# Second wide attention: GpSimd adds the two key halves of each head's weights, and the sums' product reads the added columns

## Chip, cores and metric

One core of one Trainium2 chip. The metric is device time in microseconds of one execution, median of the runs.

## The reference, cut to what matters

The kernel computes four transformer blocks on 16 sequences of 256 tokens with 128 features. The change touches the third block's attention (16 heads of 64 features, no mask):

```python
qkv = data @ W_qkv + b_qkv                    # q, k, v: [n, 256, 16, 64]
scores = jnp.einsum('nqhd,nkhd->nhqk', q, k)
attention = jax.nn.softmax(scores / 8, axis=3)
out = jnp.einsum('nhql,nlhd->nqhd', attention, v).reshape(n, l, 1024)
x = x + out @ W_out + b_out
```

The softmax is computed as weights P = exp(score/8 − max/8), the product P·V, and separately the sum of P over the keys; the output product is scaled by the reciprocal of that sum.

## The kernel before, in words

The program is a list of eight stages, each with one function per engine (`pe`, `act`, `dve`, `pool`, `sp`); the engines run their instruction lists independently and meet in semaphores. The stages are: first wide attention (`Wide`, kind 0, causal), a feed-forward net, a narrow attention, a gated net, the second wide attention (`Wide`, kind 2, s = 4, the one changed; its instructions lie at about 1,515 to 2,164 us of the profiled execution), a mixture of experts, a narrow attention, a last net.

**Units and ticks.** `Wide` cuts the work into 64 units: unit g = 4b + u holds heads 4u to 4u+3 of sequence b. The function `ticks` (line 97) writes one order for all engines by hand: a unit starts every 4 ticks, and in each tick every live unit does the part whose number `k` it has reached (`self.tk`, kind 2: "turn" 0 and 1, "v" 2, "mx" 4 and 5, "mT" 7, "st" 8 and 9, "pv" 11, "sT" 12, "out" 13). Within a tick, items are sorted by `rank` (kind 2: "turn" first part 0, "sT" 1, most others 2, "turn" second part 3, "mT" 4, dispatch 5); among equals the older unit comes first. So in one tick unit g−1 is at "out" (13) and unit g at its second "st" (9), both with rank 2. Every engine walks this one list, each doing its own share of a part.

**One unit.** TensorE makes q and k (turned), v, the score maxima ("mx") and their transpose ("mT"), then the scores with keys on partitions and queries on columns ("st", two heads per part, into PSUM [128 keys, 2 x 256 columns]: columns 0:256 are keys 0 to 127, columns 256:512 keys 128 to 255). ScalarE (line 589) writes P = exp(...) of each head as a 128x512 tile, six buffers `P` in turn. At "pv", `pe_pv` (line 438) makes P times V into `pv` (eight products, two heads side by side in the array) and then the sums' product into `sm`: eight products of `one` (128x32 of ones) with a 128x256 half of a head's P, four heads side by side, two key halves added up in PSUM. An f32 product stands in the profile as two records, so both products have 16. ScalarE copies `pv` to `OT` (line 596) and `sm` to `S` (line 599), TensorE transposes S ("sT"), VectorE takes the reciprocal (line 699). At "out", `pe_out` makes the output product from OT and `wO` into two tiles Y, VectorE scales each into a tile T (line 708), and GpSimd adds the four quarters of T into the residual XR, one after the other, each waiting for the one before (`pool_sum`, line 813; the adds are at line 825). 

**Other work in this stage.** Per sequence: statistics (VectorE lines 2419, 2421; their roots on GpSimd, lines 2426, 2428), the normalised tiles z (VectorE line 2434), the output bias added to XR (`pool_bias`, GpSimd line 811, in the tick of a "prep" with k = 3, which rank puts ahead of units), and the dispatch of the mixture of experts running behind: its own statistics and tiles zd (VectorE line 1919), gate, ranks, and two indirect DMAs issued by GpSimd (line 1973).

**Ordering between ScalarE and TensorE.** The line ahead of the exp lets ScalarE overwrite a P buffer once the sums' product of the unit that last used it is done (`filled("sm", ...)`). `take` hands out PSUM banks from a ring of eight in TensorE's order. GpSimd had no part in P in this stage.

Of the kernel before, what the change touches and what calls it, by code (L numbers as in the profile page):

```python
# [7 lines left out]
ALU = mybir.AluOpType  # L8
ACT = mybir.ActivationFunctionType
F32 = mybir.dt.float32  # L10
# [117 lines left out]
class Wide:  # L128
# [9 lines left out]
    def __init__(self, K, s, kind, loads=(), behind=None):  # L138
        self.K, self.s, self.kind = K, s, kind
        self.causal = kind == 0  # L140
        if kind == 0:
            first, last, unit = 8, 9, 23
            self.tk = {"qk": 0, "turn": 6, "mx": 9, "v": 12, "mT": 15, "st": 17, "pv": 20, "sT": 21, "out": 22}
        else:
            first, last, unit = 6, 5, 14
            self.tk = {"turn": 0, "v": 2, "mx": 4, "mT": 7, "st": 8, "pv": 11, "sT": 12, "out": 13}
        self.apart = (self.tk["st"] - self.tk["mx"]) // 4
        self.zT_at, self.sn_at = (6, 8) if kind == 0 else (4, 99)
        items = []
        for b in range(NSEQ):  # L150
            items.append((16 * b, 0, "prep", (b,), last))
            for u in range(4):
                items.append((16 * b + first + 4 * u, 1, "unit", (b, u), unit))
        if behind is not None:
            behind.ring = self.G
            items += [(16 * b + first + 12 + unit, 2, "behind", (behind, b), behind.PARTS) for b in range(NSEQ)]
        items += [(at, 3, "load", (ld,), ld.parts) for at, ld in loads]
        self.order = ticks(items, self.rank)
        sb = K.scratch
        self.zT = [sb(f"zT{s}_{i}", [128, 512], F32R) for i in range(3)]  # L160
        self.QH, self.QL, self.KH, self.KL = (
            [sb(f"{n}{s}_{i}", [128, 2, 256], F32R) for i in range(4)] for n in ("QH", "QL", "KH", "KL"))
        self.MT = [sb(f"MT{s}_{i}", [128, 256], F32R) for i in range(2)]
        self.KB = sb(f"KB{s}", [128, 8, 256] if kind == 0 else [128, 2, 128], F32R)
        self.OT = [sb(f"OT{s}_{i}", [128, 2, 256], F32) for i in range(2)]
        self.z = [sb(f"z{s}_{i}", [128, 2, 128], F32) for i in range(4 if kind == 0 else 2)]
        self.V = [sb(f"V{s}_{i}", [128, 2, 4, 64], F32) for i in range(4)]
        self.w = 384 if self.causal else 512
        self.P = [sb(f"P{s}_{i}", [128, self.w], F32) for i in range(6)]
        self.S = [sb(f"S{s}_{i}", [128, 256], F32) for i in range(2)]  # L170
        self.T = [sb(f"T{s}_{i}", [128, 2, 2, 2, 128], F32) for i in range(2)]
        self.rs = [sb(f"rs{s}_{i}", [128, 8], F32) for i in range(2)]
        self.one = sb(f"one{s}", [128, 128], F32)
        self.hi_in, self.one_in, self.summed, self.z_hi, self.kb_in = (
            K.sem(f"{n}{s}") for n in ("hi_in", "one_in", "summed", "z_hi", "kb_in"))
        if kind == 0:
            self.raw = [sb(f"raw{s}_{i}", [128, 512], F32) for i in range(6)]
            self.sqr = [sb(f"sqr{s}_{i}", [128, 512], F32) for i in range(3)]
            self.sm = [sb(f"sm{s}_{i}", [128, 64], F32) for i in range(4)]
            self.ss = [sb(f"ss{s}_{i}", [128, 48], F32) for i in range(4)]  # L180
            self.sn = [sb(f"sn{s}_{i}", [128, 64], F32) for i in range(2)]
            self.pn = [sb(f"pn{s}_{i}", [128, 2, 96], F32R) for i in range(2)]
            self.pnT = [sb(f"pnT{s}_{i}", [96, 256], F32R) for i in range(2)]
            self.nvs = sb(f"nvs{s}", [96, 2, 1040], F32R)
            self.nvo = sb(f"nvo{s}", [96, 16, 32], F32R)
            self.on = sb(f"on{s}", [128, 128], F32R)
            self.sqs, self.unitq, self.nul, self.pnull, self.rec, self.m_sm, self.nvs_in, self.snl = (
                K.sem(f"{n}{s}") for n in ("sqs", "unitq", "nul", "pnull", "rec", "m_sm", "nvs_in", "snl"))
        else:
            self.beff = sb(f"beff{s}", [1, 128], F32)  # L190
            self.bo = sb(f"bo{s}", [1, 128], F32)
            self.bias = sb(f"bias{s}", [128, 128], F32)
            self.bo_in = K.sem(f"bo_in{s}")
        K.end_scratch()
# [243 lines left out]
    def pe_pv(self, pe, g, u):  # L438


        K, s, kind, V = self.K, self.s, self.kind, self.V[g % 4]
        pv, sm = (K.ps.take(pe, self.G, name, s, g) for name in ("pv", "sm"))
        pe.wait_ge(self.one_in, 1)
        if kind == 0:
            pe.wait_ge(self.nvs_in, 4)
            pe.wait_ge(*K.ps.read("mT", s, g))
            for pr in range(2):
                c = 256 * u + 128 * pr
                K.acc(pv[:, 256 * pr:256 * pr + 256], self.nvs[:, 0, c:c + 128], self.pnT[g % 2][:, :], start=pr == 0)
            K.acc(sm[:, 0:256], self.nvo[:, 4 * u:4 * u + 4, :].rearrange("p h c -> p (h c)"), self.pnT[g % 2][:, :],  # L450
                  start=True)
        pe.wait_ge(*K.ps.read("v", s, g))
        for h in range(4):
            pe.wait_ge(*K.ps.read("st", s, g, h))
        P = [self.P[(4 * g + h) % 6] for h in range(4)]
        for pr in range(2):
            for kt, q, c, w in self.blocks():
                for par in range(2):
                    p = K.acc(pv[64 * par:64 * par + 64, 256 * pr + q:256 * pr + q + w], V[:, kt, 2 * pr + par, :],
                              P[2 * pr + par][:, c:c + w], start=kind == 2 and kt == 0 and pr == 0)  # L460
        p.then_inc(K.ps.full_of("pv", s, g), 1)
        for kt, q, c, w in self.blocks():
            for h in range(4):
                p = K.acc(sm[32 * h:32 * h + 32, q:q + w], self.one[:, 0:32], P[h][:, c:c + w],
                          start=kind == 2 and kt == 0)
        p.then_inc(K.ps.full_of("sm", s, g), 1)

    def pe_out(self, pe, g, u):
# [63 lines left out]
    def act_unit(self, ac, b, u, k):  # L532
        K, s, g, e, kind = self.K, self.s, 4 * b + u, ac.e, self.kind
        n = self.part("qk", k)
        if n is not None:
            at = 2 * g + n
# [8 lines left out]
        n = self.part("turn", k)  # L545
# [37 lines left out]
        if n is not None:  # L583
            for h in (2 * n, 2 * n + 1):
                at = 4 * g + h
                if at >= 6:
                    ac.wait_ge(*K.ps.filled("sm", s, (at - 6) // 4))
                ac.wait_ge(*K.ps.filled("st", s, g, h))
                e.activation(self.P[at % 6][:, :], K.ps.ap("st", s, g, h)[:, 0:self.w], ACT.Exp, bias=0.0,  # L589
                             scale=1.0 if kind == 0 else 0.125).then_inc(K.ps.out_of("st", s, g, h), 1)  # L590
# [191 lines left out]
    def pool(self, po):  # L782
        K, s, e = self.K, self.s, po.e
        K.stage_free(po, s)
        e.memset(self.one[:, :], 1.0).then_inc(self.one_in, 1)
        if self.kind == 0:
            for pn in self.pn:
                e.memset(fv(pn[:, :, :]), 0.0).then_inc(K.pn_in, 1)
        for name, a, k in self.order:
            if name == "prep":  # L790
                n = K.nb[s] + (4 if self.kind == 0 else 2) * a[0]
                if k == 0 or (k == 2 and self.kind == 0):
                    for i in range(2):
                        K.pool_rstd(po, n + k + i)
                if k == 3 and self.kind == 2:
                    self.pool_bias(po, a[0])
            elif name == "behind":
                a[0].pool(po, a[1], k)
            elif name == "unit":
                if self.kind == 0:  # L800
                    self.pool_unit(po, 4 * a[0] + a[1], k)
                if self.part("out", k) is not None:
                    self.pool_sum(po, *a)
            elif name == "load":
                a[0].pool(po, k)

    def pool_bias(self, po, b):
        K, x = self.K, self.K.XR[:, 2 * b:2 * b + 2, :]
        po.wait_ge(K.zs, K.nb[self.s] + 2 * b + 2)
        po.wait_ge(*K.ps.read("bias"))  # L810
        self.biased = po.step(po.e.tensor_tensor(x, x, self.bias[:, :].unsqueeze(1).to_broadcast([128, 2, 128]), ALU.add))

    def pool_sum(self, po, b, u):

# [1890 lines left out]
```

## Time and profile before

| | |
|---|---|
| median of 3 runs | 2811.08 us (2804.03 to 2811.64) |
| profiled execution, own time | 2820.46 us |
| its span | 2818.1 us |
| TensorE (PE) busy | 2493.8 us, 88% |
| VectorE (DVE) busy | 1690.2 us, 60% |
| ScalarE (ACT) busy | 1487.5 us, 53% |
| GpSimd (POOL) busy | 1455.3 us, 52% |

The rows below come from that one profiled execution; its time lies 9.4 us above the median of the runs. Matmul ends are modelled in a profile, so the distance between starts is the safer measure on PE. PE is the matmul, PEld the load of its weights. "L825" is line 825 of the kernel before. Times are microseconds unless marked ns.

### The profile page before, as it was taken

What the parts mean: (1) busy time and instruction counts of PE and PEld (TensorE: products, weight loads), DVE (VectorE), ACT (ScalarE), POOL (GpSimd) and SP (SyncE); (2) the same over time, 40 slices, a digit from 0 to 9 for tenths busy, and PEclk for the clock granted to TensorE, in tenths of its full rate; (3) what the DMA queues carried; (4) which work ended last, traced back from release to release, by engine and by line L of the source; (5) the groups of instructions that cost most, each with busy time, mean ns of one, the idle gap of its engine ahead of it and who ended that gap; (6) DMA issues with size and microseconds to landing.
All of it is one profiled execution on the core that took longest, in us unless ns stands there. A gap on an engine that the chain in (4) does not pass through costs nothing. (4 is left out here: it accounts for less than half of the span.)

```text
span 2818.1 us, 63055 instructions
## 1 busy us (share of the span) xinstructions
PE 2493.8 (88%) x24681; PEld 1914.1 (68%) x24681; DVE 1690.2 (60%) x4432; ACT 1487.5 (53%) x3177; POOL 1455.3 (52%) x2283
## 2 busy tenths in 40 slices
PE   4999999999988688889998999999996858888855
PEld 3888888888865455557777777777775745555533
DVE  4677777777757577645444666666664115555548
ACT  3666666666644476644444555555553324555531
POOL 4687777777756544434332444444443144554454
PEclk9999999999999699999999999999998977999975
DMA  3790000000000100000000000000000630000000
GB/s 107 227 325 25 2 2 2 2 2 2 2 2 1 49 2 2 2 1 21 1 1 3 3 5 5 4 6 5 6 4 16 186 97 7 7 7 3 1 1 30
DMA packets 22969, 82.68 MB, mean 29 GB/s; under 512 B 4082, under 2 KB 10868, under 8 KB 21652
## 3 DMA queue, kind: packets, MB, share of 16 engines
q1 hardware_dynamic: 19524, 71.44, 7.9%
q0 software_dynamic: 3152, 7.21, 0.8%
q8 instruction: 198, 3.24, 0.5%
q14 instruction: 95, 0.78, 0.1%
HBM read 71.44 MB, written 46.79 MB: 42 GB/s over the span
## 5 line engine op out<-in xcount | busy, mean ns | idle before, releaser
L825 POOL TENSOR_TENSOR XR<-XR,T 128x256 f32<-128x256 f32 x512 | 375.3, 733 | 441.5 <-DVE T L708 411.4
L2410 PE MATMUL ps<-P,V 128*64 128x256 f32 (+3 forms) x4096 | 341.0, 356 | 14.0 <-DVE O L1293 11.9
L589 ACT ACTIVATE P<-ps 128x384 f32<-128x384 f32 (+1 forms) x512 | 250.4, 542 | 188.6 <-PE ps L2410 188.6
L1283 DVE TENSOR_REDUCE qa<-ps 128x2 fp32r<-128x512 f32 x256 | 176.3, 689 | 219.8 <-PE ps L2410 219.7
L1206 ACT ACTIVATE P<-ps 128x768 f32<-128x768 f32 x256 | 207.5, 811 | 150.7 <-PE ps L2410 149.3
L2410 PEld LDWEIGHTS ps<-P,V 128*64 128x64 f32 (+1 forms) x4096 | 187.8, 125 | 126.1 <-issue 27.2
L2410 PE MATMUL ps<-mk,identb 128*128 128x256 bf16 (+1 forms) x1024 | 203.8, 302 | 60.4 <-DVE qa L1284 57.7
L719 DVE TENSOR_REDUCE sm<-ps 128x2 f32<-128x512 f32 (+1 forms) x256 | 130.7, 552 | 184.6 <-PE ps L2410 184.4
L1374 POOL TENSOR_SCALAR_AFFINE_SELECT P<-P 128x512 f32<-128x512 f32 x256 | 162.6, 635 | 137.2 <-ACT P L1206 137.1
L836 POOL TENSOR_TENSOR ss<-ss,nhalf 128x16 f32<-128x16 f32 x64 | 187.8, 2934 | 5.3
L2410 PE MATMUL ps<-QH,KH 64*128 64x256 f32 (+1 forms) x1024 | 165.6, 315 | 8.6 <-DVE QL L677 0.6
L2405 PE MATMUL ps<-wA,zT 128*128 128x256 f32 (+1 forms) x544 | 171.1, 314 | 1.4 <-issue 1.3
L708 DVE TENSOR_TENSOR T<-ps,rs 128x512 f32<-128x512 f32 x256 | 163.4, 679 | 8.2 <-PE ps L2410 8.2
L1547 POOL TENSOR_TENSOR hr<-hf,hr 128x512 fp32r<-128x512 f32 x64 | 82.8, 1298 | 160.9 <-DVE hr L1536 125.0
L2428 POOL TENSOR_TENSOR stat<-stat,nhalf 128x1 f32<-128x1 f32 x256 | 151.7, 593 | 21.3
L695 DVE TENSOR_REDUCE nm<-ps 128x2 fp32r<-128x512 f32 x256 | 161.7, 673 | 0.7 <-PE ps L2410 0.7
L2410 PEld LDWEIGHTS ps<-mk,identb 128*128 128x128 bf16 x1024 | 76.9, 99 | 121.7 <-DVE qa L1284 95.8
L2406 PE MATMUL ps<-wA,zT 128*128 128x256 f32 (+1 forms) x544 | 154.3, 284 | 0.0
L2407 PE MATMUL ps<-wA,zT 128*128 128x256 f32 (+1 forms) x544 | 153.2, 282 | 0.0
L596 ACT ACTIVATE OT<-ps 128x512 f32<-128x512 f32 x128 | 76.4, 597 | 136.7 <-PE ps L2410 136.7
L677 DVE SCALAR_TENSOR_TENSOR QL<-ps,par,QH 128x256 fp32r<-128x256 f32 x128 | 56.1, 480 | 154.0 <-ACT QH L557 115.1
L2410 PE MATMUL ps<-QH,KL 64*128 64x256 f32 (+1 forms) x1024 | 148.0, 278 | 0.0
(310 smaller groups left out, 7407.0 us busy)
## 6 DMA issues: line engine op xcount, KB each, us to landing
rows_i<-in_zero SPq DMA_DIRECT2D x16, 1208.0 KB, 32.2
rows_o<-in_zero SPq DMA_DIRECT2D x16, 1208.0 KB, 81.5
w<-in_m_w SPq DMA_DIRECT2D x23, 578.0 KB, 4.0
zt<-rows_i SPq DMA_DIRECT2D x23, 128.0 KB, 3.2
rows_o<-yo POOLq DMA_DIRECT2D x23, 128.0 KB, 3.9
stg<-in_t_w SPq DMA_DIRECT2D x11, 256.0 KB, 2.7
XR<-in_x SPq DMA_DIRECT2D x4, 512.0 KB, 8.4
out<-XR SPq DMA_DIRECT2D x8, 256.0 KB, 2.0
```

Source lines behind the costliest of these rows:

```text
L589: e.activation(self.P[at % 6][:, :], K.ps.ap("st", s, g, h)[:, 0:self.w], ACT.Exp, bias=0.0, scale=1.0 if kind == 0 else 0.125).then_inc(K ...
L695: e.tensor_reduce(nm[:, :, 64 * par + n], ps[:, :].rearrange("p (t c) -> p t c", t=2), X, ALU.max, negate=True).then_inc(K.ps.out_of("mx", ...
L708: e.tensor_tensor(self.T[g % 2][:, par], K.ps.ap("Y", s, g, par)[:, :].rearrange("p (a t c) -> p a t c", a=2, t=2), r[:, par].unsqueeze(3) ...
L825: p = po.e.tensor_tensor(x, x, self.T[g % 2][:, par, pr], ALU.add)
L836: d = po.step(e.tensor_tensor(ss[:, 32:48], ss[:, 16:32], K.nhalf[:, 0:16], ALU.pow))
L1206: e.activation(self.P[(2 * g + n) % 6][:, :, 0:384], K.ps.ap("st", s, g, n)[:, :, 0:384], ACT.Exp, bias=0.0, scale=self.scale).then_inc(K. ...
L1283: e.tensor_reduce(nm[:, 1], ps[:, :, 0:256], X, ALU.max, negate=True)
L1374: e.affine_select(own, own, [[0, 4], [1, 128]], ALU.is_ge, 0.0, base=0, channel_multiplier=-1).then_inc(self.masked, 1)
L2405: self.te.matmul(o, L[0], R[0], start=start, stop=False)
L2406: self.te.matmul(o, L[1], R[0], start=False, stop=False)
L2407: return self.te.matmul(o, L[0], R[1], start=False, stop=stop)
L2410: return self.te.matmul(o, l, r, start=start, stop=True, skip_group_check=True)
```

## The change

In the second wide attention only (kind 2):

- eight new buffers `PS` (128x256 f32) and a semaphore `halved`;
- a new GpSimd function `pool_halve`, called for each unit at both "st" parts, ahead of `pool_sum` of the same item but after the items of older units in that tick. For each of the two heads it waits until ScalarE has written P, and from the ninth head on for the sums' product of two units back, then adds P's columns 0:256 and 256:512 into PS and counts `halved` up;
- in `pe_pv`, after P times V, TensorE waits until all four adds of the unit are done and makes four products of `one` with PS in place of eight with P, each starting its quarter of `sm` anew;
- ScalarE's wait ahead of overwriting a P buffer is for P times V and the add of that head in place of the sums' product.

The first wide attention (kind 0) keeps its eight products and its waits.

```diff
@@ Wide.__init__
+            self.PS = [sb(f"PS{s}_{i}", [128, 256], F32) for i in range(8)]
+            self.halved = K.sem(f"halved{s}")
@@ pe_pv
-        for kt, q, c, w in self.blocks():
+        if kind == 2:
+            pe.wait_ge(self.halved, 4 * g + 4)
             for h in range(4):
-                p = K.acc(sm[32 * h:32 * h + 32, q:q + w], self.one[:, 0:32], P[h][:, c:c + w],
-                          start=kind == 2 and kt == 0)
+                p = K.acc(sm[32 * h:32 * h + 32, 0:256], self.one[:, 0:32], self.PS[(4 * g + h) % 8][:, :], start=True)
+        for kt, q, c, w in self.blocks() if kind == 0 else ():
+            for h in range(4):
+                p = K.acc(sm[32 * h:32 * h + 32, q:q + w], self.one[:, 0:32], P[h][:, c:c + w])
         p.then_inc(K.ps.full_of("sm", s, g), 1)
@@ act_unit, part "st"
-                    ac.wait_ge(*K.ps.filled("sm", s, (at - 6) // 4))
+                    ac.wait_ge(*K.ps.filled("sm" if kind == 0 else "pv", s, (at - 6) // 4))
+                    if kind == 2:
+                        ac.wait_ge(self.halved, at - 5)
@@ pool
+                n = self.part("st", k)
+                if n is not None and self.kind == 2:
+                    self.pool_halve(po, 4 * a[0] + a[1], n)
                 if self.part("out", k) is not None:
                     self.pool_sum(po, *a)
@@ new function
+    def pool_halve(self, po, g, n):
+
+        K, s = self.K, self.s
+        for h in (2 * n, 2 * n + 1):
+            at = 4 * g + h
+            if at >= 8:
+                po.wait_ge(*K.ps.filled("sm", s, g - 2))
+            po.wait_ge(*K.ps.read("st", s, g, h))
+            P = self.P[at % 6]
+            po.e.tensor_tensor(self.PS[at % 8][:, :], P[:, 0:256], P[:, 256:512], ALU.add).then_inc(self.halved, 1)
```

## Rows read from the trace of the kernel before

**Rows 1.** The page's head and its engine shares over the whole span.
```profile
span 2818.1 us, 63055 instructions
PE 2493.8 (88%) x24681; PEld 1914.1 (68%) x24681; DVE 1690.2 (60%) x4432; ACT 1487.5 (53%) x3177; POOL 1455.3 (52%) x2283
```

**Rows 2.** Windows: stretch, length, busy time per engine (instructions), granted clock, DMA.
```profile
1520.00:1560.00 40.00, 37.03 (x413) 30.14 (x412) 25.15 (x56) 24.82 (x53) 8.46 (x14) 0.99 0.01 2
1600.00:1640.00 40.00, 39.48 (x454) 31.32 (x455) 26.24 (x71) 23.29 (x51) 17.60 (x28) 1.00 0.02 5
...
2500.00:2680.00 180.00, 156.71 (x1582) 96.23 (x1582) 97.47 (x274) 102.66 (x245) 83.86 (x178) 0.91 0.01 4
```

**Rows 3.** Waits, 1620 to 2140: total us, times, longest.
```profile
POOL XR L825 <- DVE T L708: 234.9, 53, 6.8
ACT P L589 <- PE ps L2410: 98.7, 104, 1.4
```

**Rows 4.** Timeline of PE, one unit: start, us, instruction, xcount.
```profile
1606.98 1.06 PE L2410 MATMUL ps<-wO,OT 64*128 64x128 f32 x16
...
1611.18 1.95 PE L2410 MATMUL ps<-P,V 128*64 128x256 f32 x16
1613.06 1.07 PE L2410 MATMUL ps<-P,one 128*32 128x256 f32 x16
1614.06 0.44 PE L2413 MATMUL ps<-ident,nm 128*128 128x128 f32 x2
...
1616.66 1.06 PE L2410 MATMUL ps<-wO,OT 64*128 64x128 f32 x16
```

**Rows 5.** Timeline of PE, the sums' product of the next three units.
```profile
1623.33 1.07 PE L2410 MATMUL ps<-P,one 128*32 128x256 f32 x16
...
1633.68 1.07 PE L2410 MATMUL ps<-P,one 128*32 128x256 f32 x16
...
1643.36 1.07 PE L2410 MATMUL ps<-P,one 128*32 128x256 f32 x16
```

**Rows 6.** Timeline of POOL, one sequence: [idle before <- releaser].
```profile
1609.32 3.15 POOL L825 TENSOR_TENSOR XR<-XR,T 128x256 f32<-128x256 f32 x4 [6.52 <-DVE T L708]
...
1617.66 0.73 POOL L811 TENSOR_TENSOR XR<-XR,bias 128x256 f32<-128x256 f32 x1 [1.39 <-DVE z L2434]
1620.03 3.16 POOL L825 TENSOR_TENSOR XR<-XR,T 128x256 f32<-128x256 f32 x4 [1.64 <-DVE T L708]
1629.72 3.17 POOL L825 TENSOR_TENSOR XR<-XR,T 128x256 f32<-128x256 f32 x4 [6.52 <-DVE T L708]
...
1639.63 3.14 POOL L825 TENSOR_TENSOR XR<-XR,T 128x256 f32<-128x256 f32 x4 [3.01 <-DVE T L708]
1649.30 3.15 POOL L825 TENSOR_TENSOR XR<-XR,T 128x256 f32<-128x256 f32 x4 [6.53 <-DVE T L708]
```

**Rows 7.** Timeline of ACT, the weights of the unit of rows 4.
```profile
1606.94 1.09 ACT L589 ACTIVATE P<-ps 128x512 f32<-128x512 f32 x2 [0.53 <-PE ps L2410]
1609.39 1.08 ACT L589 ACTIVATE P<-ps 128x512 f32<-128x512 f32 x2 [1.37 <-PE ps L2410]
```

**Rows 8.** Timeline of DVE, the second unit of the sequence.
```profile
1617.03 0.55 DVE L2434 TENSOR_SCALAR z<-XR,stat 128x128 f32<-128x128 f32 x2
...
1618.69 0.59 DVE L1919 TENSOR_SCALAR zd<-XR,ds 128x128 f32<-128x128 f32 x2
1619.20 1.28 DVE L708 TENSOR_TENSOR T<-ps,rs 128x512 f32<-128x512 f32 x2
```

**Rows 9.** Groups of POOL by line and shape, whole span: busy us, mean ns, idle before.
```profile
L825 POOL TENSOR_TENSOR XR<-XR,T 128x256 f32<-128x256 f32 x512 | 375.3, 733 | 441.5 <-DVE T L708 411.4
L841 POOL TENSOR_TENSOR raw<-raw,ss 128x512 f32<-128x512 f32 x128 | 130.8, 1043 | 5.0
L2220 POOL TENSOR_TENSOR wS<-stg,wS 128x256 fp32r<-128x256 f32 x1 | 0.7, 742 | 0.0
```

**Rows 10.** Timeline of POOL and of DVE in the third stage.
```profile
944.71 1.26 POOL L2220 TENSOR_TENSOR wB<-stg,wB 128x512 fp32r<-128x512 f32 x1
...
943.96 0.35 DVE L2434 TENSOR_SCALAR z<-XR,stat 128x128 f32<-128x128 f32 x1 [1.98 <-POOL stat L2428]
944.84 1.21 DVE L2434 TENSOR_SCALAR z<-XR,stat 128x128 f32<-128x128 f32 x1 [0.53 <-POOL stat L2428]
```

## The prediction

> **What bounds the kernel now.** I read the page's engine shares first [rows 1]: TensorE is busy 88% of the span, GpSimd 52%. That is a mean over eight stages, so I cut the span into windows [rows 2]. The change touches the second wide attention alone (about 1,515 to 2,164 us). There TensorE is busy 39.48 of 40 us at full granted clock (1.00, the 2.4 GHz level), GpSimd 17.60. The waits of that stage [rows 3] show GpSimd waiting 234.9 us of 520 for VectorE's scaled tiles T and TensorE waiting for nobody. So today each microsecond taken from TensorE there is a microsecond of time, as long as nothing else comes to end last, and GpSimd has room on average. Whether it has room at the right moment is the question, so I laid one unit (four heads of one sequence) out in time on TensorE [rows 4] and GpSimd [rows 6].
>
> **One unit on TensorE** [rows 4]: output product of the unit before at 1606.98, then scores, projections, P times V at 1611.18, the sums' product at 1613.06, the next transposes at 1614.06, its own output product at 1616.66. Period 9.68 us. A whole sequence (four units) takes 1649.30 − 1609.32 = 39.98 us [rows 6].
>
> **Part 1, removed from TensorE.** The sums' product is 16 records in 1614.06 − 1613.06 = 1.00 us [rows 4]; 8 remain. Half is 0.50 us saved per unit, 64 × 0.50 = 32 us. If the block has a fixed part, the saving is less; it can't be over 1.00. I take 0.50; with a fixed tenth of a microsecond it would be 0.45 (3 us less in all).
>
> **Part 2, added on GpSimd.** Four adds of 128x256 f32 per unit. The nearest rows are adds of the same shape: 733 ns (L825), 730 (the bias, L811) and 742 where both inputs and the output are different tiles [rows 6, 9]. Above: 3.15/4 = 0.79, L825's pitch, but those four wait for each other and the new ones don't. Below: half of 1,043 ns, 0.52, the 128x512 multiply L841 [rows 9], whose second input is repeated, so it lies further off. I take 0.73, hence 1.44 for two in a row.
>
> **Part 3, where the adds stand in GpSimd's queue.** This decides. In the tick in which GpSimd adds heads 2 and 3 of unit g, `pool` first meets unit g−1 at its part "out": the older unit comes first, both have rank 2. So the order is: add heads 0, 1 of g; pool_sum of g−1 (3.15 us, four chained adds that wait for T); add heads 2, 3 of g. TensorE's order has the same shape: output of g−1, second scores of g, P times V of g, sums of g. For the unit shown pool_sum runs 1609.32 to 1612.47 [rows 6] and only then do the adds of heads 2, 3 start, though ScalarE has written these weights by 1609.39 + 1.08 = 1610.47 [rows 7]. They end at 1613.91; with 0.10 us for the signal the sums' product may start at 1614.01. It starts at 1613.06 now. So TensorE, so far never waiting, waits 0.95 us to save 0.50. Queued behind that wait are the transposes of the maxima, projections, scores and output product of unit g, and through them all ScalarE and VectorE work. The stall isn't made up later, because it is a loop: output of g−1 → T → pool_sum → adds → sums of g → output of g.
>
> The loop's length is a check: 1609.32 − 1606.98 = 2.34 (output to pool_sum), 3.15, 1.54 (adds and signal), 0.50 (sums), 1616.66 − 1614.06 = 2.60 (to the next output): 10.13 us, against 9.68 now and 9.18 if TensorE alone set it.
>
> **The four units of a sequence** differ. Between the end of pool_sum and the start of the sums' product there now lie [rows 4, 5, 6]: 1613.06 − 1612.47 = 0.59; 1623.33 − 1623.19 = 0.14; 1633.68 − 1632.89 = 0.79; 1643.36 − 1642.77 = 0.59. The stalls are 1.54 less these: 0.95, 1.40, 0.75, 0.95, together 4.05 us. Saved: 4 × 0.50 = 2.00. Net +2.05 us per sequence, × 16 = **+33 us**.
>
> **Adds of heads 0 and 1.** ScalarE ends their weights at about 1607.48 and 1608.03 [rows 7]; adds from 1607.6 end at 1609.05, and pool_sum starts at 1609.32. Hidden, with 0.3 us to spare; if this cover goes, all of it lands on the loop.
>
> **VectorE beside GpSimd.** Once per sequence (the second unit shown) VectorE makes two z tiles at 1617.03 and two zd tiles at 1618.69, just ahead of T at 1619.20 [rows 8], and GpSimd is idle then but for the bias add at 1617.66. After the change two adds and the bias fill about 1617.7 to 1619.9 (0.45 later for the shift). What a z tile costs beside a GpSimd add the trace shows once plainly: GpSimd's add runs 944.71 to 945.97, the z tile that starts at 944.84 takes 1.21 us instead of 0.35 [rows 10] and ends as the add ends. So a z or zd tile that comes behind an add waits for up to 0.73 us, T and with it pool_sum come that much later, in the unit with only 0.14 us of slack. One such wait per sequence is 16 × 0.73 = **+12 us**; bounds are 0 (never met) and two waits, 23 us.
>
> The Trainium skill ("SBUF — State Buffer", Who interferes with whom) has this as a rule: VectorE's fast two-port forms, or two SBUF inputs, and a GpSimd instruction hold one shared port pair by turns, and the later one blocks for the other's whole length. By that rule the 12 us belong in the sum; if it were off they would drop out and +33 would be left. Rows 10 agree with it.
>
> **Edits at no cost.** ScalarE's new waits (P times V of the unit before, and `halved`) are for adds two to three heads back, done several us earlier; the earlier release of P frees nothing that anyone waits for. Eight buffers PS and one semaphore cost no time. The adds' wait for the sums of g−2 is a period old. The first attention runs as before. Of the GpSimd work of two ticks on (the roots for z and zd, two indirect DMAs per sequence), the roots end about 1.4 us later and are still ahead of the z tiles that need them; DMAs start after the adds and end near the next heads' weights.
>
> **Sum.** 33 + 12 = +45 us. On the profiled execution's own time, 2820.46 (span 2818.1), that is 2865. That execution stands 9.4 us above the median of the three runs, 2811.08, so against the median I predict 2811 + 45 = **2856 us**. A measurement of this kernel can tell about 0.3%, 8 us, from no change.
>
> **Rivals.**
> - **No port wait, loop alone.** For it: in this stage the adds L825 (0.73) ran beside VectorE without either getting longer, and the z tiles may miss the adds by luck of timing. +33: 2844 us. Chance 0.30.
> - **Faster: TensorE stays the bound.** This needs the second pair of adds to fit the gap ahead of the sums' product. The mean gap is 0.53 us and the break-even stall 0.50, so pair and signal must take under 1.03 us, 0.46 per add or less; the adds of this shape are 0.73 to 0.74 [rows 9]. Or GpSimd would have to take heads 2, 3 ahead of pool_sum, which the tick order excludes. With all stalls gone: 2811 − 32 = 2779 us. Chance 0.07.
> - **No change:** adds at their lower bound of 0.52 take 0.40 off each stall, 26 us, which leaves 33 − 26 = +7: 2818 us. Chance 0.05.
> - **The clock falls too.** TensorE will be idle about 0.95 us in every 10.3, a busy share near 0.91. For it: in 2500 to 2680 the share is 0.87 and the granted clock 0.91 [rows 2]. Against it: at the start of this very stage the share is 37.03/40 = 0.93 with 0.99. At 0.91 the 5.4 us of TensorE-bound path in the loop (2.34 + 0.50 + 2.60) would grow by a tenth, 0.5 us × 64 = 34: 2811 + 33 + 12 + 34 = 2890 us. Chance 0.10.
> - **Not doing what it says:** if the old eight products stayed, stalls alone would give + 65; the diff guards them by kind 0, so I give this nothing.
>
> **How the numbers follow.** Forecast (loop and port) 0.48, loop alone 0.30, clock 0.10, faster 0.07, no change 0.05. The likeliest case's own range is 2845 to 2868 (port 0 to 23, saving 0.45 to 0.50). The range takes in loop alone and its error, 10 us down to 2834 (adds at 0.65), and up to 2876 for 0.79 per add (+0.12 per pair × 64 = 8) on top of two port waits; it leaves out the faster and unchanged cases and most of the clock's. Faster by over 0.3%: 0.07. Within: 0.05. Slower: 0.88.
>
> **What the profile of the changed kernel would show.** Right: TensorE waits some 0.75 to 1.4 us ahead of the sums' product, released by GpSimd's P adds, in all units but the first, 60 to 80 us in all; the stage's period per sequence is 42.0 to 42.8 us instead of 39.98; the sums' product has 8 records in about 0.5 us; GpSimd runs pool_sum and two adds back to back; zd or z tiles of up to 1 us in the second unit of a sequence. Wrong: TensorE still 98% busy there and a period near 38 us (faster rival); adds far from 0.73 us; z tiles all at 0.34 us (no port wait); a granted clock under 0.97 in 1,600 to 2,150 (clock rival); a pair of adds ahead of pool_sum.

## The result and the profile after

The changed kernel takes **2854.99 us** (median of 4 runs, 2851.3 to 2857.22), the kernel before 2811.36 us on the same chip: ratio 1.0154, interval [1.0136, 1.0172], so 43.6 us slower. The forecast was 2856 us. Lines moved by the change: the adds of T into XR are L847 (were L825), the new adds L833, the bias add L822 (L811), T is L716 (L708), zd L1941 (L1919), z L2456 (L2434), TensorE's plain products L2432 (L2410), transposes L2435 (L2413).

The page of the changed kernel, head and shares; these answer to [rows 1]:

```profile
span 2849.5 us, 62599 instructions
PE 2457.9 (86%) x24169; PEld 1890.4 (66%) x24169; DVE 1713.6 (60%) x4432; ACT 1490.1 (52%) x3177; POOL 1636.3 (57%) x2539
```

512 TensorE records fewer and 256 GpSimd instructions more: 8 records and 4 adds per unit, as written. Windows of the changed kernel, columns as in [rows 2]:

```profile
1600.00:1640.00 40.00, 35.60 (x388) 27.80 (x385) 26.07 (x66) 21.73 (x47) 27.84 (x42) 1.00 0.01 3
1600.00:2160.00 560.00, 502.45 (x5535) 397.00 (x5531) 362.89 (x905) 307.81 (x657) 380.03 (x567) 1.00 0.02 5
```

TensorE fell from 39.48 to 35.60 of 40 us busy, GpSimd rose from 17.60 to 27.84, and no engine is full. That points to a loop of waits, which the experiments below test. The granted clock stayed at 1.00. Waits of the changed kernel, 1620 to 2140 (total, times, longest), answering to [rows 3]:

```profile
POOL PS L833 <- ACT P L597: 122.7, 49, 4.4
PEld ps L2432 <- POOL PS L833: 60.6, 49, 1.7
PE ps L2432 <- POOL PS L833: 38.4, 49, 1.2
PE ps L2432 <- ACT P L597: 13.4, 49, 0.6
PEld ps L2427 <- DVE T L716: 5.2, 13, 0.4
POOL XR L847 <- DVE T L716: 15.6, 39, 0.8
```

TensorE, which waited for nobody, now waits 49 times in 520 us for the new adds, once per unit. GpSimd's 234.9 us of waiting for T shrank to 15.6. Where, is in the timeline of GpSimd:

```profile
1610.08 1.43 POOL L833 TENSOR_TENSOR PS<-P 128x256 f32<-128x256 f32 x2 [3.98 <-ACT P L597]
1611.68 3.17 POOL L847 TENSOR_TENSOR XR<-XR,T 128x256 f32<-128x256 f32 x4 [0.17 <-DVE T L716]
1614.81 1.42 POOL L833 TENSOR_TENSOR PS<-P 128x256 f32<-128x256 f32 x2
...
1654.31 3.18 POOL L847 TENSOR_TENSOR XR<-XR,T 128x256 f32<-128x256 f32 x4 [0.16 <-DVE T L716]
```

and of TensorE:

```profile
1613.58 1.95 PE L2432 MATMUL ps<-P,V 128*64 128x256 f32 x16
1616.28 0.64 PE L2432 MATMUL ps<-PS,one 128*32 128x256 f32 x8 [0.75 <-POOL PS L833]
1616.85 0.44 PE L2435 MATMUL ps<-ident,nm 128*128 128x128 f32 x2
```

Read them together: pool_sum ends at 1614.85, the adds of heads 2 and 3 at 1614.81 + 1.42 = 1616.23, the sums' product starts 0.05 us later. It lasts 0.57 us, not 1.00. One sequence now takes 1654.31 − 1611.68 = 42.63 us, not 39.98.

The same reading for all units, from the timelines of TensorE (mean distance between starts, in us, over 12 to 14 sequences between 1560 and 2140; "z unit" is the one with the z and zd tiles, the others follow it; O is the output product of the unit before, V is P times V, S the sums' product, N the transpose of the maxima):

| kernel | unit | O to V | V to S | S to N | N to next O | period |
|---|---|---|---|---|---|---|
| before | z unit | 4.78 | 1.88 | 1.00 | 3.04 | 10.71 |
| | 2nd | 4.42 | 1.88 | 1.00 | 2.60 | 9.90 |
| | 3rd | 4.20 | 1.88 | 1.00 | 2.60 | 9.68 |
| | 4th | 4.20 | 1.88 | 1.00 | 2.60 | 9.68 |
| changed | z unit | 5.21 | 3.17 | 0.57 | 3.05 | 12.00 |
| | 2nd | 4.48 | 2.47 | 0.57 | 2.61 | 10.13 |
| | 3rd | 4.57 | 2.56 | 0.57 | 2.60 | 10.30 |
| | 4th | 4.26 | 2.69 | 0.57 | 2.60 | 10.12 |

Per sequence: stalls (V to S over 1.88) 1.29 + 0.59 + 0.68 + 0.81 = 3.37; saved 4 × 0.43 = 1.72; O to V longer by 0.43 + 0.06 + 0.37 + 0.06 = 0.92. Net 2.57, × 16 = 41 us of the 43.6. The terms are not independent: where O to V grows, P times V comes later and the stall behind it is shorter. The third unit's 0.37 lengthened its period only from 10.1 to 10.30, so it is worth about 3 us and not 6.

### The profile page after: what moved, and what is told of

The parts are those of the page before. It is cut to its first block and busy times, and to the rows that moved or that the text cites. A ratio compares the mean times of both kernels' runs of the same rounds, so it can differ in the third digit from the quotient of the medians.

```text
span 2849.5 us, 62599 instructions
## 1 busy us (share of the span) xinstructions
PE 2457.9 (86%) x24169; PEld 1890.4 (66%) x24169; DVE 1713.6 (60%) x4432; ACT 1490.1 (52%) x3177; POOL 1636.3 (57%) x2539
## 5 line engine op out<-in xcount | busy, mean ns | idle before, releaser
L847 POOL TENSOR_TENSOR XR<-XR,T 128x256 f32<-128x256 f32 x512 | 376.2, 735 | 182.6 <-DVE T L716 152.5
L2432 PE MATMUL ps<-P,V 128*64 128x256 f32 (+3 forms) x4096 | 338.0, 352 | 14.1 <-DVE O L1315 11.9
L833 POOL TENSOR_TENSOR PS<-P 128x256 f32<-128x256 f32 x256 | 181.7, 731 | 177.6 <-ACT P L597 177.6
L2432 PEld LDWEIGHTS ps<-P,V 128*64 128x64 f32 (+1 forms) x4096 | 187.0, 124 | 124.3 <-issue 24.6
L2432 PE MATMUL ps<-mk,identb 128*128 128x256 bf16 (+1 forms) x1024 | 199.6, 298 | 64.0 <-DVE qa L1306 61.0
L2432 PE MATMUL ps<-QH,KH 64*128 64x256 f32 (+1 forms) x1024 | 165.7, 315 | 16.2 <-ACT P L597 16.1
L716 DVE TENSOR_TENSOR T<-ps,rs 128x512 f32<-128x512 f32 x256 | 163.4, 679 | 9.0 <-PE ps L2432 9.0
L2432 PEld LDWEIGHTS ps<-mk,identb 128*128 128x128 bf16 x1024 | 76.4, 99 | 123.7 <-DVE qa L1306 98.9
L2432 PE MATMUL ps<-QH,KL 64*128 64x256 f32 (+1 forms) x1024 | 148.1, 279 | 0.0
```

What stands on the lines that cost most here:

```text
L716: e.tensor_tensor(self.T[g % 2][:, par], K.ps.ap("Y", s, g, par)[:, :].rearrange("p (a t c) -> p a t c", a=2, t=2), r[:, par].unsqueeze(3) ...
L833: po.e.tensor_tensor(self.PS[at % 8][:, :], P[:, 0:256], P[:, 256:512], ALU.add).then_inc(self.halved, 1)
L847: p = po.e.tensor_tensor(x, x, self.T[g % 2][:, par, pr], ALU.add)
L2432: return self.te.matmul(o, l, r, start=start, stop=True, skip_group_check=True)
```

## Experiments

Two theories. **Loop**: the time is lost because the adds of heads 2 and 3 stand behind pool_sum, in a loop through TensorE. **Volume**: 181 us more GpSimd work, or its contention with VectorE, slows the stage wherever it stands. Ratios are against the kernel before on the same chip, whose medians there were 2803 to 2806 us.

### e1: the smaller product alone

```diff
-        for kt, q, c, w in self.blocks():
+        for kt, q, c, w in self.blocks()[:1 if kind == 2 else 2]:
```

> The kernel before, with the sums' product reading columns 0:256 of each head's P alone, without any GpSimd add (keys 128 to 255 are left out of the softmax sum). It measures the term 'removed from TensorE' by itself. Loop theory (TensorE is the bound as long as it needn't wait): the block of the sums' product shrinks from 1.00 to 0.57 us as in the changed kernel, 64 x 0.43 = 27.5 us, 2784 us; if the block had no fixed part it would be 32 us, 2779. Rival (the stage is not bound by TensorE's products, another engine ends last close behind): less than 10 us gained.

Measured 2779.85 us, ratio 0.9911 [0.9895, 0.9928]: 25 us gained. Its sums' product takes 0.57 us, and TensorE is still busy 394.66 of 400 us there (1700 to 2100). So the saving is 0.43 per unit (27.5 us), not half of 1.00: eight records take 0.57 and sixteen 1.00, which leaves a fixed 0.14. TensorE does set the time when nothing makes it wait.

### e2: the adds, unused

The changed kernel with the eight old products and no wait for the adds; ScalarE waits for the old product and `halved`.

> The changed kernel with the adds on GpSimd, but TensorE makes the eight old products and doesn't wait for the adds. It measures what the adds cost merely by being on GpSimd. Loop theory: only the zd tiles blocked behind adds and bias (0.4 us once per sequence, at most 6.6 us) can show: 2811 to 2818 us. Rival (the loss comes from 181 us more GpSimd work and its contention with VectorE, not from the wait): most of the +44 us stays, over 2835 us.

Measured 2814.46 us, ratio 1.0035 [1.0022, 1.0047]: 10 us, a little over the 0 to 7 expected. The volume theory needed most of 44. The timelines of e2, read as for the table, say where the 10 are: O to V is 5.21, 4.48, 4.26, 4.26, so 0.43 in the z unit and 0.06 in each other, together 0.61 × 16 = 9.8 us. VectorE's timeline in e2, z unit:

```profile
1616.52 0.55 DVE L2453 TENSOR_SCALAR z<-XR,stat 128x128 f32<-128x128 f32 x2
1618.19 1.01 DVE L1938 TENSOR_SCALAR zd<-XR,ds 128x128 f32<-128x128 f32 x2
1619.12 1.27 DVE L713 TENSOR_TENSOR T<-ps,rs 128x512 f32<-128x512 f32 x2
```

The zd pair takes 1.01 us, not 0.59 [rows 8]; T and all behind it come 0.42 later. The 0.06 is ScalarE's second wait: the idle time before the exps is 0.59 us, not 0.53 [rows 7]:

```profile
1606.43 1.09 ACT L594 ACTIVATE P<-ps 128x512 f32<-128x512 f32 x2 [0.59 <-PE ps L2429]
```

### e3: the wait with the old product

> The changed kernel with the wait for the adds kept, but all eight old products of P made after it. Loop theory: the block is 1.00 instead of 0.57 us and stands in the loop behind the wait, so the whole 0.43 comes on top, 64 x 0.43 = 27.5: 2855 + 27 = 2882 us. Rival (the wait hides part of the product, for instance because TensorE preloads weights): under 2870 us.

The edit puts `pe.wait_ge(self.halved, 4 * g + 4)` ahead of the eight old products. Measured 2871.04 us, ratio 1.0239 [1.0223, 1.0255], against 1.0154: about 24 us more than the changed kernel (sequence 44.05 us against 42.55). The product's 0.43 is worth its full length behind the wait too; nothing of it hides. It is a little under the 27.5, because the longer O to V of the third unit (4.57) is 4.26 here; its period grew by 0.24 and not by 0.43.

### e4: adds first

```diff
-                n = self.part("st", k)
-                if n is not None and self.kind == 2:
-                    self.pool_halve(po, 4 * a[0] + a[1], n)
+                g, n = 4 * a[0] + a[1], self.part("st", k)
+                if self.kind == 2 and n is not None and (n == 0 or g == 0):
+                    self.pool_halve(po, g, n)
                 if self.part("out", k) is not None:
+                    if self.kind == 2 and g + 1 < 4 * NSEQ:
+                        self.pool_halve(po, g + 1, 1)
                     self.pool_sum(po, *a)
```

> The changed kernel with one thing moved: GpSimd adds heads 2 and 3 of unit g ahead of pool_sum of unit g-1 (same tick, other order). Loop theory: P of heads 2, 3 is written 3.5 us after the output product starts, so both adds end at 4.5 us and TensorE wants them at 6.1; no wait, the gain of the smaller product stays: 2811 - 27 = 2784 us, with up to 10 us lost where the roots, the bias and the zd tiles now come later. Rival (GpSimd as a whole is too slow, or pool_sum becomes late by the 1.4 us and delays VectorE's T and the dispatch): 2811 us or more.

Measured 2793.78 us, ratio 0.9968 [0.9955, 0.9981]. The same work in another order on one queue is 1.8% faster than the changed kernel. V to S is 1.88 in all four units: no stall. But 9 us gained is short of the 17 to 27 expected: O to V is 5.56 in the z unit. GpSimd and VectorE there:

```profile
1614.77 0.57 POOL L1991 TENSOR_TENSOR ds<-ds,nhalf 128x1 f32<-128x1 f32 x1
1615.31 1.43 POOL L835 TENSOR_TENSOR PS<-P 128x256 f32<-128x256 f32 x2
1616.70 0.73 POOL L824 TENSOR_TENSOR XR<-XR,bias 128x256 f32<-128x256 f32 x1
```

```profile
1615.44 1.39 DVE L1943 TENSOR_SCALAR zd<-XR,ds 128x128 f32<-128x128 f32 x2
1616.74 1.28 DVE L716 TENSOR_TENSOR T<-ps,rs 128x512 f32<-128x512 f32 x2
```

The four roots end later, so the adds of heads 0 and 1 run exactly beside the zd tiles. Both tiles are blocked now, and the pair takes 1.39 us.

### e5: two heads only

Heads 0 and 1 go through PS (ahead of pool_sum), heads 2 and 3 keep two products each.

> Only heads 0 and 1 of each unit are added on GpSimd (ahead of pool_sum, where they are covered); heads 2 and 3 keep their two products each. Six products in place of eight, no adds behind pool_sum, so by the loop theory no wait: the stall of 60 us vanishes. If the block's time goes by the number of products it is 0.86 us and saves 0.14 x 64 = 9 us; if it goes by the deepest of the four column groups (two products for heads 2 and 3, as before) it saves nothing. With up to 10 us for zd tiles and the exps' extra wait: time of before, -9 to +10 us. Rival (the loss is from having GpSimd in the path at all): over +20 us.

Measured 2811.48 us, ratio 1.0031 [1.0017, 1.0046]. The stall is gone, and so is the saving: from the first record (1610.70) to the next transposes (1611.70) it is 1.00 us, with 12 records in place of 16:

```profile
1610.70 0.41 PE L2433 MATMUL ps<-PS,one 128*32 128x256 f32 x2
1610.71 0.41 PE L2433 MATMUL ps<-P,one 128*32 128x256 f32 x2
...
1611.70 0.44 PE L2436 MATMUL ps<-ident,nm 128*128 128x128 f32 x2
```

The four heads' products run side by side in four column groups, and the block lasts as long as the group with most products. A gain needs all four heads. The 0.3% lost is mostly the zd pair again: O to V of the z unit is 5.21, so 0.43 × 16 = 7 us.

### e6: the bias add later

```diff
-                if k == 3 and self.kind == 2:
+                if k == 4 and self.kind == 2:
                     self.pool_bias(po, a[0])
```

> The changed kernel with the bias add on GpSimd one tick later, behind the adds of heads 2 and 3, so that it no longer stands beside the zd tiles. In the changed kernel the two zd tiles take 1.01 us in place of 0.59 and the bias add 0.81 in place of 0.73. Port theory: zd back to about 0.6, T and with it TensorE 0.4 us earlier once per sequence, 16 x 0.4 = 6.6 us: ratio to before 1.013 in place of 1.0154. Rival (zd is late for another reason, such as the roots): no change, 1.0154.

Measured 2835.48 us, ratio 1.0109 [1.0087, 1.0131], against 1.0154: about 12 us better. In the changed kernel GpSimd and VectorE do this in the z unit:

```profile
1620.21 1.45 POOL L833 TENSOR_TENSOR PS<-P 128x256 f32<-128x256 f32 x2 [0.57 <-ACT P L597]
1621.62 0.81 POOL L822 TENSOR_TENSOR XR<-XR,bias 128x256 f32<-128x256 f32 x1
1621.49 1.01 DVE L1941 TENSOR_SCALAR zd<-XR,ds 128x128 f32<-128x128 f32 x2
```

and in e6:

```profile
1619.19 1.44 POOL L833 TENSOR_TENSOR PS<-P 128x256 f32<-128x256 f32 x2 [0.58 <-ACT P L597]
1620.47 0.59 DVE L1941 TENSOR_SCALAR zd<-XR,ds 128x128 f32<-128x128 f32 x2
1620.98 1.28 DVE L716 TENSOR_TENSOR T<-ps,rs 128x512 f32<-128x512 f32 x2
```

With the bias add the pair ends at 1622.50, just after that add (1622.43); without it zd is back to 0.59, though it begins 0.16 us before the adds of heads 0 and 1 end (1620.63). O to V of the z unit goes from 5.21 to 4.78, the value before: 0.43 × 16 = 6.9 us, the term in question. Counted in periods the z unit gives 0.50 (12.00 to 11.50), 8 us, and the third unit 0.20 (10.30 to 10.10), 3 us: its O to V fell from 4.57 to 4.25, and part of that came back as a longer stall. Which wait makes it 4.57, the traces don't settle: in the changed kernel ScalarE's exps start about 0.4 us late in most third units, behind scores that were long done,

```profile
1684.64 1.09 ACT L597 ACTIVATE P<-ps 128x512 f32<-128x512 f32 x2 [1.02 <-PE ps L2432]
```

and in no other run do they. So this delay need not belong to the bias add.

### e7: adds first, bias later, one wait

e4 and e6 together, and ScalarE's two waits ahead of the exp replaced by the old single one (`filled("sm", ...)`, which implies the adds).

> e4 (adds of heads 2, 3 ahead of pool_sum) with the bias add one tick later and ScalarE waiting once per exp: for the sums' product of the unit that used the buffer (which itself waited for that unit's adds) in place of two waits. e4 gained 9 us, the smaller product alone 25. Theory: of the 16 us lost, 0.06 x 64 = 4 us are the second wait ahead of the exp, and part of the 0.8 us per sequence by which the zd tiles are late (1.39 in place of 0.59 us) is the bias add: ratio 0.993 to 0.996 against 0.9968 of e4. Rival (the rest of the loss is GpSimd's four roots delaying the adds): no change from 0.9968.

Measured 2784.48 us, ratio 0.9938 [0.9921, 0.9956]: 17 us under the kernel before and some 60 under the changed one, with the full computation. O to V is 5.34 in the z unit and 4.42, 4.20, 4.20 after it, the values of before; the remaining 0.56 per sequence is the zd pair, 1.23 us beside the adds of heads 0 and 1.

### e8: one wait

The changed kernel with ScalarE's single wait.

> The changed kernel with ScalarE waiting for the sums' product of the buffer's last user alone, as before the change (that product itself waits for the adds, so the wait for the adds is implied), in place of two waits. In every trace with two waits the exps start 0.06 us later behind their scores and TensorE then waits for them ahead of the second scores. Theory: 0.06 x 64 = 4 us of the change's 44: ratio 1.0140. In the loop it may be less, since the adds of heads 2, 3 wait for pool_sum and not for the exps, but pool_sum waits for the output product that follows them. Rival (the 0.06 us is absorbed by the stall): 1.0154.

Measured 2845.78 us, ratio 1.0158 [1.0143, 1.0174]: no difference from 1.0154. The rival was right. The exps do start earlier (O to V 4.19, not 4.26), and the stall is that much longer (V to S 2.73, not 2.69; period of the fourth unit 10.10 and 10.12): in a loop that runs through GpSimd, TensorE's slack is worth nothing.

### e9 and e10: the same two extra adds, in two places

`pool_extra` makes two more 128x256 adds per unit (of ones, into a buffer that nobody reads): in e9 behind the adds of heads 2 and 3, in e10 between pool_sum and those adds.

> The changed kernel with two more 128x256 adds per unit on GpSimd (of ones, into a buffer that nobody reads), placed behind the adds of heads 2 and 3, where GpSimd is idle in three units of four. Loop theory: off the loop, 0 to 16 us more than the changed kernel (in the unit with the four roots the next adds and the bias come up to 1 us later, once per sequence): ratio 1.0154 to 1.021. Rival (GpSimd's total work or its contention with VectorE sets the time): 64 x 1.4 = 90 us more, 1.047.

> The same two extra adds per unit, placed between pool_sum and the adds of heads 2 and 3. Loop theory: they lie in the loop, each unit's stall grows by their whole 1.41 us, 64 x 1.41 = 90 us more than the changed kernel: ratio 1.0154 + 0.032 = 1.047. Rival (total work): the same as e9.

Measured: e9 2847.52 us, ratio 1.0151 [1.0118, 1.0184]; e10 2987.39 us, ratio 1.0643 [1.0609, 1.0677]. 90 us more GpSimd work costs nothing behind the adds and 138 us between. Windows of e9 and then of e10:

```profile
1620.00:2140.00 520.00, 469.44 (x5162) 370.19 (x5158) 342.86 (x849) 287.01 (x614) 418.97 (x625) 1.00 0.02 5
```

```profile
1620.00:2140.00 520.00, 424.35 (x4272) 338.68 (x4273) 286.48 (x696) 238.00 (x509) 346.07 (x517) 0.92 0.01 4
```

This settles the two theories: e9 has GpSimd busy 419 of 520 us and no loss. e10 lost more than its 90 us, and more than was expected of it. At full clock its unit period is the expected one, 10.12 + 1.4 (TensorE's output products at 1616.63 and 1628.08, 11.45 us apart). But over these 520 us the granted clock averages 0.92 (between its two levels, 1.2 and 2.4 GHz), after waits of about 2 us per unit for the adds. Three stretches around two such waits (S at 1738.77 and at 1753.07):

```profile
1738.80:1743.40 4.60, 4.60 (x38) 3.86 (x40) 1.21 (x5) 1.60 (x4) 2.98 (x8) 0.63 0.00 0
1743.50:1753.10 9.60, 6.69 (x74) 5.12 (x73) 6.41 (x12) 4.72 (x10) 7.75 (x11) 1.00 0.01 2
1753.10:1759.50 6.40, 6.40 (x42) 5.26 (x44) 2.03 (x9) 1.67 (x5) 0.00 (x0) 0.50 0.00 0
```

The clock falls in the stretch between the sums' product and the next output product, in every second unit: N to next O is 4.10 there in place of 2.60, and 5.48 in place of 3.05 in every second z unit. Two sequences (1743.45 to 1845.87) take 51.2 us each, 8.65 more than in the changed kernel. Of these, 5.46 are longer V to S, 87 us in the stage, as expected; 3.45, 55 us, are N to next O, which the lower clock takes (0.50 is the 1.2 GHz level), 0.22 is the product itself, and O to V is 0.48 shorter. No run held the clock up with these waits in place. TensorE's timeline in e10:

```profile
1616.63 1.06 PE L2442 MATMUL ps<-wO,OT 64*128 64x128 f32 x16
...
1624.91 0.64 PE L2442 MATMUL ps<-PS,one 128*32 128x256 f32 x8 [2.09 <-POOL PS L839]
1628.08 1.06 PE L2442 MATMUL ps<-wO,OT 64*128 64x128 f32 x16
```

## Why the prediction was right

**The decisive step** held: the tick order puts pool_sum ahead of the adds of heads 2 and 3, and with them 3.15 + 1.4 us of chained GpSimd work into TensorE's loop. e4 (order alone, no stall) and e9 against e10 (place alone, 0 against 138 us) show it.

**Saved on TensorE**: 0.50 per unit predicted, 0.43 measured (e1, table); the text's own alternative of a fixed tenth was nearer. That is 28 us, not 32.

**Adds**: 0.73 taken, 0.731 measured, two in a row about 1.41.

**Stalls**: 4.05 us per sequence predicted, 3.37 measured. The signal took 0.05 us, not the 0.10 that was taken without a row for it, the pair 1.41, not 1.44, and where O to V grew, P times V itself came later and so waited less. Predicted 60 to 80 us in all, found 54: this term was over-sized by 11 us.

**Cover of heads 0 and 1**: held. Their adds end at 1611.51, pool_sum starts at 1611.68, released by T.

**VectorE beside GpSimd**: 0.73 per sequence predicted, 0.43 measured (12 and 7 us). One of the two zd tiles is blocked, not for a whole add but for what was left of it. e6 takes the term away with the bias add. By the rule of the Trainium skill ("SBUF — State Buffer", Who interferes with whom) the later of the two blocks until the first has ended. The traces agree, and they show that the wait's length depends on where in the add the tile arrives: 1.01 for the pair here, 1.23 in e7, 1.39 in e4, where both tiles are blocked, and none in e6, where zd began 0.16 us before the adds ended.

**Priced at nothing, and wrong**: ScalarE's added wait. It puts the exps 0.06 us later (e2's O to V), about 3 us where TensorE is the bound; in the changed kernel it is absorbed (e8). And O to V of the third unit, 0.37 per sequence or 6 us, was not foreseen; half of it only took the place of a stall, and its cause is open.

So the sum, +45 against +43.6, is better than its terms: 33 from stalls and saving turned out 26, the port term 12 turned out 7, and 8 us came from terms that the text had at zero; 2 to 3 us lie outside the units read. The mechanism was right, but the agreement to 1.4 us is luck: errors of 3 to 11 us in single terms cancelled.

**Rivals.** Loop alone (+33) fell because a zd tile did wait (e2, e6), though the term is smaller than the 12 us by which the two forecasts differ. Faster and unchanged fell with the adds' measured 0.73. The clock did not fall: it stayed at 1.00 with the changed kernel's waits of 0.6 to 1.3 us per unit. In this stage it fell only in e10 (0.92), where they are about 2 us.

## What to carry to other kernels

Before moving work to an engine with spare time, write down what stands ahead of it in that engine's queue at the moment when its result is due: the share of busy time said 52%, and 0.6 us of slack behind a 3.15 us chain decided. Where the engines share one hand-written order, put the short task that the bound engine waits for ahead of the long one that nobody waits for (e7: 0.9938 with the same adds, against 1.0154). Products that run side by side in column groups get shorter only if the deepest group does.

## What the runs showed that was not expected

- A second semaphore wait ahead of a ScalarE instruction delays its start by 0.06 us even when both are long met (idle before the exps 0.59 against 0.53 in e2 and the kernel before). It showed only because TensorE takes the bank of these exps for its next scores.
- Small VectorE operations of the dispatch were blocked too. In the changed kernel, beside the adds of heads 2 and 3:

```profile
1637.52 0.44 DVE L1976 CAST place<-dg 128x2 int32<-128x2 f32 x1
1638.06 0.58 DVE L1979 TENSOR_TENSOR hots<-hots,hot 128x8 bf16<-128x8 bf16 x1
```

  They take 0.17 and 0.16 us in the kernel before. The cast takes 0.44 in every sequence; the second is blocked in this one of 13 sequences only (mean 0.19), but in every sequence of e4, e7 and e9 (means 0.71, 0.71 and 0.58). The indirect DMAs wait for the cast's result. No run took these delays away, so what they cost is not shown.
- Eight f32 products in four column groups take 1.00 us, four take 0.57, and six with two groups still two deep 1.00.
